# A six-layer windowed-attention decoder on one core: exponentials straight from PSUM, weights ahead, and a new order

## What is computed

```python
def local_attention(q, k, v):            # windows of 32 queries
    bk2, bv2 = (look(bk), look(bv))      # each with its own and the window before: 64 keys
    sim = jnp.einsum('bhwie,bhwje->bhwij', bq, bk2) * QK_SCALE
    sim = jnp.where(mask, -jnp.finfo(sim.dtype).max, sim)
    attn = jax.nn.softmax(sim, -1)
    out = jnp.einsum('bhwij,bhwje->bhwie', attn, bv2)

def attn_layer(x, Wqkv, qs, ksc, Wo):
    q, k, v = jnp.split(x @ Wqkv, 3, -1)          # 128 -> 3 x 1024
    q = l2norm(q) * qs;  k = l2norm(k) * ksc      # per head
    q = q * cos * scale + rotate_half(q) * sin * scale
    k = k * cos / scale + rotate_half(k) * sin / scale
    return local_attention(q, k, v) @ Wo

def ffn_layer(x, g, bln, W1, b1, W2, b2):
    xn = layernorm(x) * g + bln
    a, gate = jnp.split(xn @ W1 + b1, 2, -1)      # 2 x 341
    return a * jax.nn.gelu(gate) @ W2 + b2

for i in range(6):
    x = attn_layer(shift_tokens(x), ...) + x
    x = ffn_layer(shift_tokens(x), ...) + x
```

## Time and profile before

| | us |
|---|---|
| median of 3 runs | 1827.44 (1825.43 to 1829.06) |
| the profiled execution | 1832.19 |
| its span (first to last instruction) | 1830.4 |
| PE matmuls busy | 1636.3 (89%) |
| DVE busy | 1537.4 (84%) |
| POOL busy | 1361.2 (74%) |
| ACT busy | 1188.8 (65%) |
| chain that ended last | PE 74%, issue 5%, DVE 4% |
| mean granted TensorE clock | 0.954 of full speed |

### The profile page before, as it was taken

One profiled execution on the slowest core, in us unless ns is written; L12 is line 12 of the kernel. 1 busy time (PEld: TensorE's weight loads), 2 busy tenths in 40 slices (PEclk: granted clock), 3 DMA queues, 4 the chain that ended last, 5 costly groups with the idle time before them and its releaser, 6 DMA issues.

```text
span 1830.4 us, 77270 instructions
## 1 busy us (share of the span) xinstructions
PE 1636.3 (89%) x32727; PEld 1367.4 (75%) x32727; DVE 1537.4 (84%) x3220; ACT 1188.8 (65%) x2281; POOL 1361.2 (74%) x971
## 2 busy tenths in 40 slices
PE   6688769999989999989999989999899999899985
PEld 4455557788777888878887878888788888788873
DVE  6588779988878999879998979999799899799951
ACT  4465546676666777657767756777676677577651
POOL 4355567788767888778887878888688888788852
PEclk9789979999999999999999999999999999999996
DMA  3644211111221212111213112112112131121101
GB/s 102 253 162 162 81 48 34 41 43 39 92 55 34 54 46 82 53 51 43 54 40 101 40 46 56 47 58 86 43 40 54 40 112 41 45 56 47 37 18 52
DMA packets 81081, 118.47 MB, mean 65 GB/s; under 512 B 41643, under 2 KB 55140, under 8 KB 80612
## 3 DMA queue, kind: packets, MB, share of 16 engines
q1 hardware_dynamic: 80162, 113.27, 21.0%
q10 hardware_dynamic: 578, 0.26, 0.1%
HBM read 38.72 MB, written 21.32 MB: 33 GB/s over the span
## 4 chain that ended last, share of the span: by engine, by line
PE 74%; issue 5%; DVE 4%; DMA 1%; ACT 1%; POOL 1%; SPq 0%; ACTq 0%; DVEq 0%; POOLq 0%
PE banks L1168 10%; PE banks L1181 10%; PE banks L1086 8%; PE banks L1130 7%; PE banks L1088 7%; PE banks L1087 7%; PE banks L1143 5%; PE banks L1098 4%; PE banks L1108 4%; PE banks L1223 4%; PE banks L1198 2%; PE banks L1200 2%; PE banks L1199 2%; DMA wo<-in_L_ffn_Wo_dram 1%; PE banks L1069 1%
## 5 line engine op out<-in xcount | busy, mean ns | idle before, releaser
L1416 POOL TENSOR_TENSOR qk_c<-qk_c,qk_s 128x1024 f32<-128x1024 f32 x192 | 459.2, 2392 | 210.9 <-DVE qk_s L1511 208.1
L1424 POOL TENSOR_TENSOR qk_c<-qk_c,nrm 128x1024 f32<-128x1024 f32 x192 | 362.6, 1905 | 41.0 <-DVE nrm L1559 41.0
L1086 PE MATMUL banks<-high,xT 128*128 128x512 f32 x576 | 270.9, 470 | 19.4 <-DVE qk_s L1511 12.1
L1500 DVE TENSOR_TENSOR qk_c<-banks,rot 128x512 f32<-128x512 f32 x384 | 261.6, 681 | 31.1 <-ACT sq L1289 30.0
L1329 ACT COPY pT<-banks 128x512 f32<-128x512 f32 x192 | 112.7, 587 | 266.2 <-PE banks L1143 266.2
L1511 DVE TENSOR_TENSOR qk_s<-banks,rot 128x512 f32<-128x512 f32 x384 | 261.2, 680 | 0.0
L1289 ACT ACTIVATE sq<-banks 128x512 f32<-128x512 f32 x384 | 237.0, 617 | 23.3 <-PE banks L1088 13.3
L1088 PE MATMUL banks<-high,xT 128*128 128x512 f32 x576 | 231.6, 402 | 0.9 <-issue 0.9
L1518 DVE TENSOR_REDUCE ssq<-sq 128x16 f32<-128x1024 f32 x192 | 232.0, 1208 | 0.0
L1087 PE MATMUL banks<-low,xT 128*128 128x512 f32 x576 | 230.2, 400 | 0.9 <-issue 0.9
L1181 PEld LDWEIGHTS banks<-wo,attT 128*128 128x128 f32 x1536 | 194.9, 200 | 36.5 <-issue 26.3
(11 more groups left out here) (157 smaller groups left out, 3673.7 us busy)
## 6 DMA issues: line engine op xcount, KB each, us to landing
v_back<-v_own SPq DMA_DIRECT2D x96, 384.0 KB, 3.7
front_raw<-in_L_ffn_Wqkv_dram SPq DMA_DIRECT2D x18, 512.0 KB, 5.5
v_back<-v_own SPq DMA_DIRECT2D x72, 128.0 KB, 2.4
w_high<-high SPq DMA_DIRECT2D x15, 512.0 KB, 2.7
w_low<-low SPq DMA_DIRECT2D x15, 512.0 KB, 4.1
high<-w_high SPq DMA_DIRECT2D x15, 512.0 KB, 4.7
low<-w_low SPq DMA_DIRECT2D x15, 512.0 KB, 4.9
wo<-in_L_ffn_Wo_dram SPq DMA_DIRECT2D x6, 512.0 KB, 5.1
```

Of the source, the lines that this page charges most:

```text
L1086: pe.matmul(bank[n % 2][:, :], xT[:, 1, lo:lo + P], w_hi[:, col:col + 512], start=True, stop=False)
L1416: pool.tensor_tensor(x, x, qk_s[:, kind, :], ALU.add).then_inc(s["rotd"], 1)
L1424: pool.tensor_tensor(x, x, bcast(nrm[:, t % 2, HEADS * kind:HEADS * (kind + 1)], 2, DH), ALU.mult).then_inc(s[("qn", "kn")[kind]], 1)
L1500: dve.tensor_tensor(qk_c[:, t % 2, kind, 512 * half:512 * half + 512].rearrange("p (h d) -> p h d", d=DH), bank[n % 2][:, :].rearrange("p ...
```

## The change

- `exponentials` reads the scores from banks 4 and 5 and subtracts the maximum by its bias: 16 instructions of 64 columns a tile, for 2 of 512. `score_max` writes the negated maximum (two buffers `nmax`), `score_sub` and `sdif` are gone. The scores' banks are free after the exponentials.
- `attend` writes to banks 6 and 5, no longer 6 and 3.
- `wo` has two buffers and is loaded a layer ahead (tile 5 of the layer before). Of the rotary tables two layers lie in SBUF; the other four are stored to memory at the end of `front` and loaded a layer ahead. The layer norm's weights have a semaphore of their own, and the feed-forward weights are waited for at the first gate, and issued at tile 10 of a layer and not at tile 9.
- The projections have two semaphores, one for each bank.
- In the last two rows the feed-forward's steps use banks 0 to 5 and 7 (`ffn_bank`). The last sum is taken by row ahead of the last feed-forward (`sum_rows`), whose output is added into it, and the result is stored by row.
- The order of all bodies is new. Queries, probabilities and attention output keep a single buffer.

The core of the diff (the four bodies at its end are PE's, ACT's, POOL's and DVE's):

```diff
-            rot=sb("rot", [P, DEPTH, 4, GPB * DH]),
+            rot=sb("rot", [P, 2, 4, GPB * DH]),
+            rot_d=nc.dram_tensor("tables", [DEPTH, P, 4 * GPB * DH], F32, kind="Internal").ap(),
...
+            for layer in range(2, DEPTH):
+                sp.wait_ge(s_const, 2 * layer + 2)
+                sp.dma_start(k["rot_d"][layer, :, :], later[:, layer - 2].rearrange("p k n -> p (k n)")).then_inc(s_tabout, 16)
             sp.wait_ge(s_skip, 16 * BATCH)
+            sp.wait_ge(s_tabout, 16 * (DEPTH - 2))
...
-    wo = sb("wo", [P, PAIRS, D])
+    wo = sb("wo", [P, 2, PAIRS, D])
-    smax = sb("smax", [P, HEADS])
-    sdif = sb("sdif", [P, 2 * 512])
+    nmax = sb("nmax", [P, 2, HEADS])
...
+    def ffn_bank(r, job):
+
+        if r == NIT - 2:
+            return {"gate0": 0, "gate1": 0, "gate2": 0, "value0": 1, "value1": 1, "value2": 1}.get(job, 7)
+        if r == NIT - 1:
+            return {"gate0": 0, "gate1": 2, "gate2": 4, "value0": 1, "value1": 3, "value2": 7, "out": 5}.get(job, 7)
+        return 7
...
-                    if layer > 0 and at == 4:
-                        sp.wait_ge(s["wo_p"], BATCH * GPB * layer)
-                        load_wo(layer)
-                    if layer > 0 and at == 9:
+                    if layer + 1 < DEPTH and at == 5:
+                        need(sp, s["wo_p"], BATCH * GPB * layer)
+                        load_wo(layer + 1)
+                    if 2 <= layer + 1 < DEPTH and at == 6:
+                        sp.wait_ge(s["ab"], 4 * BATCH * GPB * layer)
+                        sp.dma_start(rot[:, (layer + 1) % 2].rearrange("p k n -> p (k n)"), k["rot_d"][layer + 1, :, :]).then_inc(s["rot_in"], 16)
+                    if layer > 0 and at == 10:
...
-                bank_turn(4, "dif", t + 1)
-                bank_turn(5, "dif", t + 1)
+                bank_turn(4, "ex", 2 * t + 1)
+                bank_turn(5, "ex", 2 * t + 2)
...
-                to = (6, 3)
+                to = (6, 5)
...
             def body(it, j, t):
+                transpose_k(t - 2, 0)
+                transpose_k(t - 2, 1)
+                if j == 1:
+                    ffn_value(it - 3, 2)
+                if j == 0:
+                    ffn_gate(it - 3, 2)
+                project(t, 2)
+                if j == 2:
+                    ffn_out(it - 3)
+                transpose_prob(t - 3, 0)
+                if j == 0:
+                    ffn_value(it - 3, 0)
+                scores(t - 2)
+                transpose_x(t + 1)
+                transpose_prob(t - 3, 1)
+                project(t, 3)
+                project(t, 4)
+                out_proj(t - 4)
+                project(t + 1, 0)
+                transpose_q(t - 1, 0)
                 if j == 0:
                     ffn_value(it - 3, 1)
+                if j == 3:
+                    ffn_gate(it - 2, 0)
+                project(t, 5)
+                transpose_q(t - 1, 1)
+                attend(t - 3)
                 if j == 3:
                     ffn_gate(it - 2, 1)
+                project(t + 1, 1)
+                if j == 2:
+                    ffn_transpose(it - 2)
...
-                act.wait_ge(s["dif"], t + 1)
+
+                act.wait_ge(s["maxed"], t + 1)
                 need(act, s["pT_p"], 2 * t - 3 + half)
-                act.activation(prob[:, t % 2, 512 * half:512 * half + 512], sdif[:, 512 * half:512 * half + 512],
-                               ACT.Exp).then_inc(s["ex"], 1)
+                for g in range(8):
+                    at = 512 * half + 64 * g
+                    last = act.activation(prob[:, t % 2, at:at + 64], bank[4 + half][:, 64 * g:64 * g + 64], ACT.Exp,
+                                          bias=nmax[:, t % 2, 8 * half + g:8 * half + g + 1])
+                last.then_inc(s["ex"], 1)
...
             def body(it, j, t):
+                copy_x(t + 1)
+                shift_x(t)
+                store_prob(t - 4, 1)
+                squares(t - 1, 3)
+                store_values(t - 1, 0)
+                exponentials(t - 3, 0)
+                exponentials(t - 3, 1)
+                store_q(t - 2, 0)
+                if j == 0:
+                    store_gate(it - 3, 0)
+                squares(t, 0)
+                store_values(t - 1, 1)
+                if j == 1:
+                    store_value(it - 3, 1)
+                store_q(t - 2, 1)
+                store_att(t - 4, 0)
+                if j == 0:
+                    store_gate(it - 3, 1)
+                squares(t, 1)
+                store_att(t - 4, 1)
+                store_k(t - 2, 0)
+                if j == 0:
+                    store_gate(it - 3, 2)
+                store_k(t - 2, 1)
+                squares(t, 2)
+                if j == 1:
+                    store_value(it - 3, 2)
+                if j == 0:
+                    store_value(it - 3, 0)
                 if j == 3:
+                    ffn_normT(it - 2)
                 store_prob(t - 3, 0)
...
             def body(it, j, t):
+                rotate(t - 1, 1)
+                normalise_prob(t - 3, 0)
+                normalise_prob(t - 3, 1)
...
+                low_x(t + 2)
                 normalise(t - 1, 0)
+                rotate(t, 0)
                 normalise(t - 1, 1)
...
             def body(it, j, t):
                 square_sum(t - 1, 0)
+                root_step(t - 2, 5)
+                cos_part(t - 1, 1)
+                root_step(t - 2, 6)
+                sin_part(t - 1, 1)
+                root_step(t - 2, 7)
+                cos_part(t - 1, 2)
+                if j == 3:
+                    add_ffn(it - 3)
+                root_step(t - 2, 8)
+                sin_part(t - 1, 2)
+                root_step(t - 2, 9)
                 score_mask(t - 3)
                 score_max(t - 3)
                 cos_part(t - 1, 3)
                 sin_part(t - 1, 3)
+                add_attention(t - 5)
                 square_sum(t - 1, 1)
...
                 prob_sum(t - 3)
+                cos_part(t, 0)
+                prob_inv(t - 3)
+                sin_part(t, 0)
                 root_step(t - 1, 0)
...
                 root_step(t - 1, 4)
```

More of the change, by code:

```diff
@@ L195, in front @@
     table = sb("table", [P, 4, GPB * DH])
+    later = sb("later", [P, DEPTH - 2, 4, GPB * DH])
     qscl = sb("qscl", [P, DEPTH, DH])
@@ L352, in scaled_tables @@
                     pool.tensor_tensor(
-                        rot[:, layer, 2 * n:2 * n + 2, :].rearrange("p k (j d) -> p (k j) d", d=DH),
+                        (rot[:, layer] if layer < 2 else later[:, layer - 2])[:, 2 * n:2 * n + 2, :].rearrange(
+                            "p k (j d) -> p (k j) d", d=DH),
                         table[:, 2 * n:2 * n + 2, :].rearrange("p k (j d) -> p (k j) d", d=DH),
@@ L997, in load_next @@
             def load_next(layer, n):
-                sp.wait_ge(s["proj"], NPROJ * (BATCH * GPB * (layer + 1) - 1) + 2 * n + 2)
+                for proj in ("proj0", "proj1"):
+                    sp.wait_ge(s[proj], 3 * (BATCH * GPB * (layer + 1) - 1) + n + 1)
                 load(layer + 1, n)
@@ L1180, in out_proj @@
                 for c in range(PAIRS):
-                    last = pe.matmul(bank[7][:, 0:D], attT[:, c, :], wo[:, c, :], start=(c == 0), stop=(c == PAIRS - 1))
+                    last = pe.matmul(bank[7][:, 0:D], attT[:, c, :], wo[:, t // (BATCH * GPB) % 2, c, :], start=(c == 0), stop=(c == PAIRS - 1))
                 last.then_inc(s["wo_p"], 1)
@@ L1222, in ffn_out @@
                         m += c == 2
[L1223 removed]
+                        last = pe.matmul(bank[b][:, P * t:P * t + P], f_h[0:m, c, P * t:P * t + P], w2[0:m, c, :],
                                          start=(c == 0), stop=(c == 2))
@@ L1354, in store_gate @@
                 need(act, s["w2_p"], r)
-                act.activation(f_h[0:m, c, :], bank[7][0:m, :], ACT.Gelu, bias=b1c[0:m, 3 + c:4 + c]).then_inc(s["fg"], 1)
+                act.activation(f_h[0:m, c, :], bank[ffn_bank(r, f"gate{c}")][0:m, :], ACT.Gelu, bias=b1c[0:m, 3 + c:4 + c]).then_inc(s["fg"], 1)
             def store_value(r, c):
@@ L1362, in store_value @@
                 need(act, s["fh"], 3 * r + c - 1)
-                act.activation(f_v[0:m, c % 2, :], bank[7][0:m, :], ACT.Identity, bias=b1c[0:m, c:c + 1]).then_inc(s["fv"], 1)
+                act.activation(f_v[0:m, c % 2, :], bank[ffn_bank(r, f"value{c}")][0:m, :], ACT.Identity,
+                               bias=b1c[0:m, c:c + 1]).then_inc(s["fv"], 1)
             def body(it, j, t):
-                if j == 3:
-                    store_gate(it - 2, 0)
-                store_att(t - 4, 0)
```

198 lines of the change are left out of this document (68 added, 130 removed).

## The result

| | before | after |
|---|---|---|
| median of 4 runs | 1828.25 us | 1917.11 us |
| profiled execution | 1832.2 us (span 1830.4) | 1912.7 us (span 1910.8) |
| forecast | | 1801 us (1768 to 1862) |

The ratio is 1.047 (95% interval 1.039 to 1.055). The change costs 89 us where a gain of 26 was forecast, and the time lies outside the range.

A forecast was written before the change was run, and what follows sets the result against it. PE and DVE were taken to bind a quiet row together, with room on ACT. Rows +12, `wo` ahead -40, layer weights +4, first stage's end +7 and tail -9 gave -26 us, from 1827.4 to 1801 (range 1768 to 1862).

The forecast's parts named there:

- PE's short breaks: Pauses of PE inside the attention matmuls, estimated at 0.2 us a round, making a row 61.8 us, as before.
- The ring of 14.07 us: Loop of exponentials, attention matmuls, attention copy, DVE's root steps and products, mask and maximum: 14.07 us a round.
- The exponential at 0.21 us: Each 64-column exponential with a column bias holds ACT 0.21 us; sixteen take 3.45 us a round.
- The rival of dear exponentials: Small exponentials take 0.25 us each, giving 1863 us, or 0.24, giving 1844; chance 0.20 for the two.
- The feed-forward's share: Table loads, Gelus and output matmuls add +1.6, +1.4, +0.2 and +1.5 us, taking four rounds from 56.3 to 61.0.
- A row of 61.8 + 0.5: Four rounds with feed-forward and PE's breaks take 61.8 us, plus 0.5 for missed waits: +12 us in all.
- too careful: Rival: PE's breaks fall into slack and nothing else is missed, 61.0 us a row, 1770 us; chance 0.15.
- Seam, +4: At layer changes, single-buffered value weights land late: +0.8 us a layer, +4 in all.
- The rival of weights that are late by 8 us: Value or query weights come late by the 8 us that `wo` was, five times: 1837 us; chance 0.08.
- End of the first stage, +7: Four 512 KB tables stored behind the last residual must land before the stage ends: +7 us, between +4 and +9.
- Tail, -9: Last row's up-projections with a bank each -5 us, last sum off the path -2.3, smaller last store -1.8.
- The rival of a wait that was missed, 2 us a row: The new order has an overlooked wait of 2 us in each row: 1837 us; chance 0.10.

The follow-up runs named there:

- `a_full`: Changed kernel with two windows per small matmul in scores and attention (half of both results wrong), dummy transposes restoring burst length: 1751 us, ratio 0.955.
- `b_wo`: Kernel before with only the output weights `wo` double-buffered and loaded a layer ahead: 1797 us, ratio 0.982.
- `b_wo_end`: Kernel before with `wo` loaded a layer ahead and the changed kernel's end (`ffn_bank`, `sum_rows`): 1786 us, ratio 0.975.
- `b_nops`: Kernel before, meant to get 48 no-operations per tile on TensorE; its trace has only 24 instructions more in all: 1875 us, ratio 1.022.
- `a_sub`: Changed kernel with the subtraction on DVE and two exponentials of 512 columns a tile back: 1858 us, ratio 1.013.

## Why the prediction was wrong, step by step

- *The step that failed* is the one on PE's short breaks: "0.2 a round (an estimate): 61.8, as before", 19 us in all, with 0.5 a row beside it for missed waits, 12 us more. The pauses of before were seen and taken as a fixed part of attention. They are stands at borders, which depend on how close the bursts lie. In the changed kernel they are 4.8 us a row (114.4 / 24), and their whole effect 6.9 (166 / 24). In the old order attention to scores was 6.3 us and scores to attention 4.1; in the new one 3.3 to 5.5 and 7.0, and attention's stands fall on the ring. Term: 31 forecast, 166 measured. In the old kernel it was 77 already (50.9 us of stands), which the 0.2 a round had too low as well.
- *The ring of 14.07 us*: right. In the changed kernel's trace rounds without feed-forward and stands, from one run of exponentials to the next, take 13.79 and 14.07; the run itself is 3.39 us for 3.45.

```profile
923.07 3.39 ACT L1349 ACTIVATE prob<-banks,nmax 128x64 f32<-128x64 f32 x16
```

- *The exponential at 0.21 us*: right, the starts are 0.196 apart. The rival of dear exponentials falls. So does the estimate of 0.24 from the figures of the Trainium skill, "ScalarE: Activation LUTs", section "What ACT_TABLE_LOAD costs". Of the expected signs some hold: DVE waits before the sum of probabilities, 77.6 us in total, and PE before attention, 0.65 to 0.8 us in a third of the tiles. ACT is busy 53.1 us of a row (55.6 forecast), but of a longer one: 79% and not 88.

```profile
L1614 DVE TENSOR_REDUCE psm<-prob 128x16 f32<-128x1024 f32 x96 | 117.1, 1220 | 77.7 <-ACT prob L1349 77.6
```

- *The feed-forward's share*: right, once packets are in time. The four rounds of a quiet row in `a_full` take 13.8, 16.9, 14.1 and 15.2 us, where the sum has 14.07, 17.1, 14.07 and 15.6. In the changed kernel the round of the stand shown above took 21.15 and a later one, of the other kind, 17.15. Each holds one stand of 1.6 to 1.7 inside attention; the first also holds 6.8 us at 1.2 GHz (matmuls of 512 columns that start 0.43 apart instead of 0.23).
- *A row of 61.8 + 0.5, against 61.8 before*: with packets in time the new row is 60.0, so the sum without the breaks (61.0) was 1 us a row too high, 24 us. But the old row is 58.9 then. The forecast compared a sum with a measured row that had its own late packets in it, and so it missed that the new order and the exponentials together make a row 1.1 us longer. Its gain of 26 us would not have come with packets in time either; the rival "too careful", with 57 us of gain, still less.
- *`wo` ahead, -40*: right, 35 us (`b_wo`).
- *Seam, +4*: of the right size; PE's own waits for these weights are 3.4 us in five layers. The rival of weights that are late by 8 us falls, although the chain shows 6.5 us for them.
- *End of the first stage, +7*: the first transposes of the stack start 4.3 us later, the first attention 8.8.
- *Tail, -9*: 6.5 in the changed kernel, 11 in `b_wo_end` against `b_wo`.
- *The rival of a wait that was missed, 2 us a row*, is the nearest in kind: the chance was 0.10 and the price less than half of what came. The range had no room for a resource that the busy rows do not show.

Left open: why a packet starts 3 to 6 us late after two close borders; how the 166 us split between the stands (114), the clock (63 at most) and the ring behind them, and the 77 likewise (51, 10 at most, and the rest); and whether a shift of the borders by a few instructions would save the changed kernel what one cost `b_nops`.

## What to carry over

Count TensorE's instructions and divide by 256 before trusting its busy time: where borders fall within some 4.6 us of each other, a pause at the next may come (28 of 44 cases here, 18 of 59 in the old order), of 1.7 us in the median (1.1 in the old order), and a reorder that packs dense bursts closer, or puts them on a ring without slack, can turn pauses that cost little into time. And a measured row is no clean base for a sum that leaves such pauses out: both sides need the same terms. Prices of such pauses belong to the order, not to the instruction, so they are not carried from one order to another as "as before". And try parts of a change alone: two of the four here (`wo` ahead and the end) bring 2.5% in the old order, while the exponentials cost 107 us there. The new order was not run alone: with the loads and the end, but without the small exponentials, it took 1858 us (`a_sub`), where the old order with `wo` ahead and the end takes 1786.

## What the hardware showed that was not expected

- TensorE's program comes in 16 KB packets, one per 256 instructions; the packet takes 1.0 us, PE went on 2.1 us or more after its start, and 67,132 instructions against 44,476 are worth 77 us in one order and 166 in the other.
- 24 instructions more in 67,132, with the same work and order, changed the time by 45 us (2.2%) in one kernel and by nothing clear (-5) in the other, by the place of the borders. A difference of 1 to 2% between two orders of such a kernel may be nothing else.
- The granted clock goes with the stands: 33 falls to 1.2 GHz in the changed kernel's stack, 25 of them at a stand, and 3 falls in `a_full`, which has no stands.
- Exponentials of 64 columns with a column as bias follow each other at 0.196 us.
